# A decoder layer on one Trainium2 core: masked scores kept in PSUM, transposes ahead of scores, and a rebuilt passage from the last head group into attention

## What is computed

```
x = layernorm(x + mamba(x))                      # 8 groups of 16 heads; each group normed by its own mean square
x = layernorm(x + attention(x, ctx, ctx, mask))  # queries x, keys and values ctx
x = layernorm(x + (silu(x @ Wg.T) * (x @ Wu.T)) @ Wd.T)

def attention(q, k, v, mask):                    # 32 query heads of 16, 8 key heads
    scores = einsum('bsgrd,btgd->bgrst', q, k) / sqrt(16) + mask
    probs = softmax(scores, axis=-1)
    return einsum('bgrst,btgd->bsgrd', probs, v)
```

## Time and profile before

| | us |
|---|---|
| median of 3 runs | 1650.11 (1648.63 to 1650.75) |
| the profiled execution | 1650.3 |
| its span | 1648.6 |
| PE busy | 1612.6 (98%) |
| DVE busy | 1197.8 (73%) |
| ACT busy | 950.9 (58%) |
| POOL busy | 962.6 (58%) |

### The profile page before, as it was taken

The page is one execution under the profiler, slowest core; times in us unless marked ns, Lnnn a source line. Parts: engine busy times, 40 slices in busy tenths (PEclk is TensorE's granted clock), DMA queues, the critical chain, the costliest instruction groups (busy, mean ns, idle before and its releaser), DMA issues.

```text
span 1648.6 us, 25601 instructions
## 1 busy us (share of the span) xinstructions
PE 1612.6 (98%) x9120; PEld 1271.4 (77%) x9120; DVE 1197.8 (73%) x2366; ACT 950.9 (58%) x1584; POOL 962.6 (58%) x727
## 2 busy tenths in 40 slices
PE   8999999999999999999999999999999997889998
PEld 7788888888888888888888888888888884444646
DVE  7767688767877786768686868586858679996433
ACT  6765377446745583558364837384738365995231
POOL 2977478657956694759474948495938563330000
PEclk9999999999999999999999999999999999999999
DMA  5432133213412241224131423142314182000000
GB/s 187 148 114 78 58 103 134 77 58 102 132 61 78 90 135 58 90 85 134 53 101 61 135 74 103 53 140 62 119 45 135 58 107 106 1 20 20 13 14 26
DMA packets 76547, 138.85 MB, mean 84 GB/s; under 512 B 6786, under 2 KB 13954, under 8 KB 76164
## 3 DMA queue, kind: packets, MB, share of 16 engines
q1 hardware_dynamic: 76420, 137.21, 26.5%
HBM read 134.55 MB, written 2.63 MB: 83 GB/s over the span
## 4 chain that ended last, share of the span: by engine, by line
PE 90%; DVE 6%; issue 1%; ACT 1%; DMA 1%; POOL 0%; SPq 0%; DVEq 0%; POOLq 0%; ACTq 0%
PE ps_hs L248 8%; PE ps_hs L250 8%; PE ps_hs L249 8%; PE ps_gate L249 8%; PE ps_gate L248 8%; PE ps_gate L250 8%; PE ps_y L1199 7%; PE ps_hs L1207 7%; PE ps_hs L1208 7%; PE ps_hs L1209 7%; PE ps_gate L1183 4%; PE ps_y L1487 3%; PE ps_hs L1449 3%; PE ps_dec L1449 3%; DVE pr L1030 2%
## 5 line engine op out<-in xcount | busy, mean ns | idle before, releaser
L765 DVE SCALAR_TENSOR_TENSOR conv<-ps_hs,cw,conv 128x508 f32<-128x508 f32 (+2 forms) x432 | 320.1, 741 | 31.5 <-ACT conv L530 20.2
L394 POOL TENSOR_TENSOR cum_bc<-cum_bc,neg_cum 128x1024 f32<-128x1024 f32 x128 | 247.5, 1934 | 10.8 <-DMA cum_bc<-cum_scratch 0.2
L248 PE MATMUL ps_hs<-x_hi,w_hi 128*128 128x512 f32 x576 | 231.4, 402 | 0.0
L250 PE MATMUL ps_hs<-x_hi,w_lo 128*128 128x512 f32 x576 | 225.2, 391 | 0.0
L248 PE MATMUL ps_gate<-x_hi,w_hi 128*128 128x512 f32 x576 | 224.4, 390 | 0.0
L249 PE MATMUL ps_hs<-x_lo,w_hi 128*128 128x512 f32 x576 | 224.3, 389 | 0.0
L249 PE MATMUL ps_gate<-x_lo,w_hi 128*128 128x512 f32 x576 | 224.3, 389 | 0.0
L250 PE MATMUL ps_gate<-x_hi,w_lo 128*128 128x512 f32 x576 | 224.3, 389 | 0.0
L1207 PE MATMUL ps_hs<-wo_hi,g_hi 128*128 128x512 f32 x488 | 190.3, 390 | 0.0
L1209 PE MATMUL ps_hs<-wo_hi,g_lo 128*128 128x512 f32 x488 | 190.0, 389 | 0.0
L1208 PE MATMUL ps_hs<-wo_lo,g_hi 128*128 128x512 f32 x488 | 189.9, 389 | 0.0
(11 more groups left out here) (172 smaller groups left out, 3240.6 us busy)
## 6 DMA issues: line engine op xcount, KB each, us to landing
cum_bc<-cum_scratch SPq DMA_DIRECT2D x128, 512.0 KB, 4.2
w_raw<-w_in SPq DMA_DIRECT2D x145, 256.0 KB, 4.7
wo_raw<-w_out SPq DMA_DIRECT2D x64, 256.0 KB, 5.0
g_acc<-x_t SPq DMA_DIRECT2D x4, 512.0 KB, 6.8
acc<-x_nat SPq DMA_DIRECT2D x1, 2048.0 KB, 10.1
k_rep<-ctx_t SPq DMA_DIRECT2D x8, 256.0 KB, 12.9
out<-y_out SPq DMA_DIRECT2D x8, 256.0 KB, 2.0
wg_sb<-w_gate SPq DMA_DIRECT2D x1, 1792.0 KB, 17.2
```

Of the source, the lines that this page charges most:

```text
L248: eng.matmul(ps, whi, xhi, start=(k == 0), stop=False)
L250: return eng.matmul(ps, wlo, xhi, start=False, stop=(k == n - 1))
L394: gp.tensor_tensor(part, part, start.broadcast_to([P, 2, HB, SEQ]), ALU.add).then_inc(S["bc_ok"], 1)
L765: v.scalar_tensor_tensor(out=dst, in0=src, scalar=cw[:, at, TAPS - 1 - n:TAPS - n], in1=dst, op0=ALU.mult, op1=ALU.add).then_inc(S["tap"], 1)
```

## The change

**Scores.** `masked` writes back into its own score bank instead of `pr`, and `exponentials` reads there and writes `pr`. So the bank is free only after the exponential: `scores(i)` waits for `p_exp` of i - 2, half by half, where it waited for `s_max` of i - 2.

**Order.** In the loop PE issues `values` and `turn_probs` ahead of `scores`; ACT issues `keep_queries` after the first half's exponentials instead of before; `scores(0)` stands ahead of the last batch's `last_products`.

**Statistics.** `first_stats` of batches 2 to 7 move from before the loop into its iterations 0 to 5, and `second_part(7)` into iteration 0 between the two halves. The reciprocal roots, other than of batches 0 and 1 and of the last norm, are now made on POOL (`powers`: add EPS, then a power of -0.5) inside its loop of `k_bd`; ACT's roots with their table loads go, and one small exponential loads the table ahead of the loop.

**Last group.** `earlier_squares` moves up behind the last output products, into `ps_dec[0]`, and `last_squares` up in front of most products; the first sum is taken early, the mask is negated early.

```
@@ DVE, ahead of the loop
+            dve.wait_ge(S["ss_early"], 1)
+            v.tensor_scalar(rstd_g[:, :], ps_dec[0][:, 0:BATCH], 1.0 / (TPG * P), EPS, ALU.mult, ALU.add)\
+                .then_inc(S["ss_part"], 1)
+            dve.wait_ge(S["m3_in"], 16)
+            v.tensor_scalar(mask_sb[:, :], mask_sb[:, :], -1.0, None, ALU.mult).then_inc(S["m3_neg"], 1)
+            dve.wait_ge(S["ss_part"], 1)
             dve.wait_ge(S["ss_ps"], GROUPS)
-            v.tensor_scalar(rstd_g[:, :], ps_y[0][:, 0:BATCH], 1.0 / (TPG * P), EPS, ALU.mult, ALU.add)\
-                .then_inc(S["ss_part"], 1)
...
-            for n in range(2):
-                normed(1, n, acc[:, n, :]).then_inc(S["x1_ok"], 1)
-            for b in range(3, 6):
+            normed(1, 0, acc[:, 0, :]).then_inc(S["x1_ok"], 1)
+            for b in range(3, 5):
                 first_part(b)
                 second_part(b)
+            normed(1, 1, acc[:, 1, :]).then_inc(S["x1_ok"], 1)
+            first_part(5)
+            second_part(5)
             first_part(6)
             first_part(7)
-            first_stats(2)
             second_part(6)
-            first_stats(3)
-            second_part(7)
-            for b in range(4, BATCH):
-                first_stats(b)
-            variances(1, 1, others)
@@ DVE, in the loop
             def masked(i, par):
                 dve.wait_ge(S["s_ps"], 2 * i + par + 1)
-                need(dve, S["pt_ps"], 2 * (i - 3) + par + 1)
+                need(dve, S["p_exp"], 2 * (i - 3) + par + 1)
                 for r in range(REP):
                     n = par * REP + r
+                    one = S_PS[i % 2][par][:, r * SEQ:(r + 1) * SEQ]
                     last = v.tensor_tensor_reduce(
-                        out=pr[i % 3][:, n, :], in0=S_PS[i % 2][par][:, r * SEQ:(r + 1) * SEQ], in1=mask_sb[:, :],
+                        out=one, in0=one, in1=mask_sb[:, :], scale=1.0, scalar=FAR, op0=ALU.add, op1=ALU.min,
...
                     masked(i, 0)
+                    if i == 0:
+                        second_part(7)
                     masked(i, 1)
-                if i == 1:
-                    inverses(1, 1, others)
+                if i + 2 < BATCH:
+                    first_stats(i + 2)
@@ ACT
             def exponentials(i, par):
                 act.wait_ge(S["s_max"], 2 * i + par + 1)
+                need(act, S["pt_ps"], 2 * (i - 3) + par + 1)
-                    e = sc.activation(pr[i % 3][:, n, :], pr[i % 3][:, n, :], ACT.Exp, scale=-1.0,
-                                      bias=neg_max[:, i % 3, n:n + 1])
+                    e = sc.activation(pr[i % 3][:, n, :], S_PS[i % 2][par][:, r * SEQ:(r + 1) * SEQ], ACT.Exp,
+                                      scale=-1.0, bias=neg_max[:, i % 3, n:n + 1])
...
-            root(1, 1, slice(2, BATCH))
+            sc.activation(rstd[2][:, 0:1], ones[:, 0:1], ACT.Exp).then_inc(S["exp_table"], 1)
...
-                if i == 23:
-                    root(2, 0, slice(0, HB))
...
-                    if hf == 0 and m == 3:
-                        root(2, 1, slice(HB, BATCH))
@@ POOL
+            def powers(stage, cols):
+                pool.wait_ge(S[f"mv{stage}"], cols.stop)
+                gp.tensor_scalar(rstd[stage - 1][:, cols], mv[stage - 1][:, cols, 1], EPS, None, ALU.add)\
+                    .then_inc(S[f"eps{stage}"], 1)
+                pool.wait_ge(S[f"eps{stage}"], 1 + (cols.stop == BATCH))
+                gp.tensor_tensor(rstd[stage - 1][:, cols], rstd[stage - 1][:, cols], minus_half[:, cols], ALU.pow)\
+                    .then_inc(S[f"pow{stage}"], 1)
...
+                if i == 3:
+                    powers(1, slice(2, HB))
+                if i == 7:
+                    powers(1, slice(HB, BATCH))
+                if i == 24:
+                    powers(2, slice(0, HB))
...
+            powers(2, slice(HB, BATCH))
@@ PE
             outputs(t, 1)
+            earlier_squares(t)
             pe.wait_ge(S["wo_lo_ok"], t)
-            last_products((0, 1, 2, 3), (2,))
-            earlier_squares(t)
+            last_products((0,), (2,))
             last_squares(t)
...
             def scores(i):
-                need(pe, S["s_max"], 2 * (i - 2) + 2)
                 for par in range(2):
+                    need(pe, S["p_exp"], 2 * (i - 2) + par + 1)
```

More of the change, by code:

```diff
@@ L409, in _ @@
             gp.tensor_copy(ones_r[:, :], ones[:, :]).then_inc(S["ones_r_ok"], 1)
+            gp.memset(minus_half[:, :], -0.5).then_inc(S["half_ok"], 1)
+            pool.wait_ge(S["half_ok"], 1)
             def split_squares(g):
@@ L1117, in _ @@
                         batch_done(BATCH - 1)
-                        variances(2, 1, second_half)
                     if m == 4:
-                        inverses(2, 1, second_half)
+                        dve.wait_ge(S["pow2"], 2)
                     if m in (4, 5):
@@ L1267, in earlier_squares, with last_squares @@
                 pe.wait_ge(S["sq_add"], 2 * t)
+                for b in range(BATCH):
+                    mm = pe.matmul(ps_dec[0][:, b:b + 1], sq_acc[:, b * SEQ:(b + 1) * SEQ], ones[:, 0:1],
+                                   start=True, stop=True)
+                mm.then_inc(S["ss_early"], 1)
+            def last_squares(t):
+                pe.wait_ge(S["sq_ok"], 2 * t + 2)
                 pe.wait_ge(S["g_lo_ok"], 2 * t + 1)
                 for b in range(BATCH):
-                    pe.matmul(ps_y[0][:, b:b + 1], sq_acc[:, b * SEQ:(b + 1) * SEQ], ones[:, 0:1],
-                              start=True, stop=True)
-            def last_squares(t):
-                pe.wait_ge(S["sq_ok"], 2 * t + 2)
-                for b in range(BATCH):
-                    mm = pe.matmul(ps_y[0][:, BATCH + b:BATCH + b + 1],
+                    mm = pe.matmul(ps_y[0][:, b:b + 1],
                                    sq_tmp[:, b // HB, (b % HB) * SEQ:(b % HB + 1) * SEQ], ones[:, 0:1],
@@ L1418, in _ @@
             last_products((6,), range(TPH))
+            pe.wait_ge(S["rstd_v"], GROUPS)
+            scores(0)
             pe.wait_ge(S["gacc_ok"], kept + 4)
@@ L1421, in _ @@
             pe.wait_ge(S["v_ok"], 1)
-            pe.wait_ge(S["rstd_v"], GROUPS)
-            scores(0)
             pe.wait_ge(S["gacc_ok"], kept + 6)
@@ L1427, in _ @@
                     pe.wait_ge(S["gacc_ok"], kept + BATCH)
-                if i + 1 < CHUNKS:
-                    scores(i + 1)
                 if i % 2 and i >= 5:
@@ L1433, in _ @@
                     turn_probs(i - 2)
+                if i + 1 < CHUNKS:
+                    scores(i + 1)
                 if i % 2 and i >= 7:
@@ L1452, in hidden @@
                     mm.then_inc(S[done], 1)
-            pe.wait_ge(S["s_max"], 2 * CHUNKS)
+            pe.wait_ge(S["p_exp"], 2 * CHUNKS)
             pe.wait_ge(S["x2_lo_ok"], HB)
```

29 lines of the change are left out of this document (14 added, 15 removed).

## The result

The changed kernel is slower by 0.3%: 1654.15 us, median of 7 runs (1652.77 to 1658.19), against 1649.12 of before in the same comparison (7 runs). The ratio is 1.003 with a 95% interval of 1.002 to 1.0039. In all that follows two executions that ran slow at a lower granted clock (2709.19 us of e7_first, 1802.77 of e11_best) are left out of medians and ratios.

What follows compares the result with a forecast made beforehand. Three nearly full engines were taken to hold each other up in the attention loop; 1370.2 + 101.3 + 2.6 + 2.5 put the last mask at 1476.6, 8.1 us earlier, giving 1642.0 us, range 1638.5 to 1649.

Steps and rivals of the forecast that it cites:

- Part 1: Last sums of squares ahead of the loop: sum ready 1.65 us earlier, one small operation gone, 1.9 us in all.
- Part 2: DVE up to the first mask: statistics and small work leave, 6.35 us saved; first mask at 1370.2.
- Part 3: ACT in the loop: exponentials from PSUM 0.04 us shorter, table loads gone; work per batch from 12.7 to 11.3 us.
- Part 4: DVE in the loop bounds next: 101.3 us of work, plus 10 ns per PSUM mask, 2.6 us for 256.
- Rival 3: DVE's PSUM masks in the loop each cost 20 to 40 ns more: 1644.5 to 1649.5 us, chance 0.12.
- Part 5: Score ring and PE's queue in the loop: 3 us of slack, DVE idle 2.5 us in place of 10.0.
- the note on POOL: POOL in the loop: 4.16 us of work in 13.9, small operations 1 to 2 us ahead of need; cost 0.
- POOL's power: Power instruction on POOL, without a row: up to 1.5 us each covered, cost taken as 0.
- DVE's list: DVE's loop work by kind: 95.5 us before, 101.3 with six statistics and batch 7's addition.
- The stretch behind the last mask: From last mask to the FFN's first matmul: 7.1 us of turned probabilities and split x2, unchanged.
- The rule named in the prediction: Memory latency shows between VectorE and ScalarE instructions; by it ACT's saving is real and DVE's 256 short masks pay each time.

Runs made afterwards that it cites:

- e7_first: Changed kernel with masked scores back in SBUF, bank freed by the mask, and PE's old loop order (scores ahead of values and transposes): 1644.4 us, ratio 0.9971.
- e11_best: Changed kernel with masked scores in SBUF, POOL's key blocks beside the masks, and three products instead of one between the sums of squares: 1640.7 us, ratio 0.9946.
- e4_order: Changed kernel with PE's loop order undone: scores ahead of values and transposes, PSUM output and release by the exponentials kept: 1713.6 us, ratio 1.0385.
- e8_table: Changed kernel with a table of DVE operations, alone and beside POOL, behind its last store: 1692.2 us, of which only the table's rows count.
- e2_keys: Changed kernel with one more wait on POOL, so its key blocks are multiplied beside DVE's masks: 1647.7 us, ratio 0.9992.
- e1_sbuf: Changed kernel with masked scores back in SBUF, exponentials in place there and the score bank freed by the mask: 1641.8 us, ratio 0.9963.
- e10_share: Changed kernel, masks still in PSUM, with key blocks beside masks, three products between squares, and ACT copying half 1 of every fourth piece: 1646.1 us, ratio 0.9978.
- e9_bboth: Kernel before with the scores part alone: masks in PSUM, scores released by both halves' exponentials, values and transposes ahead of scores: 1664.1 us, ratio 1.0089.

## Why the prediction was wrong, step by step

Two steps failed. The price of the mask's output in PSUM was put at 10 ns and measured 31 on average (5.7 us in all), and POOL's multiplications beside DVE's operations in SBUF had no term at all (6.8 us). A smaller one is the clock at the last squares (1.4 us). The last mask was to end at 1476.6 and ended at 1490.07, 13.5 us later. The terms:

- **Part 1 (last squares), size wrong.** The additions were to start 1.9 us earlier, at 1354.2; they started at 1355.57, 1.4 us late. The order of work did what was said. The run of e4_order, where the clock held through the second set, has the step at 2.86, 1.98 less than before. I took the 1.93 us of the earlier trace rows for a set that now stands nearly alone behind another, and did not ask what clock it would have.
- **Part 2 (DVE up to the first mask), right.** From first addition to first mask 15.83 us; 1370.2 less 1354.2 is 16.0. With part 1's error the first mask came at 1371.4.
- **Part 3 (ACT), right.** Exponentials from PSUM stand 0.25 us apart instead of 0.29, ACT is busy 12.18 in 15.0 us and waits for DVE (13.3 us in 13 waits in the loop). Worth what the next engine lets through, as it said.
- **Part 4 (DVE late next), right on the engine and wrong on two sizes.** The bound is DVE, full. The price of the mask was put at 10 ns from a plain multiplication in place, 19 ns in the earlier trace rows. That row was true for what it showed, and e8_table finds no price on a plain addition; but the mask is another kind of instruction, and its price was 38 ns from one to the next, 31 on average since the first of a row of masks has none (in the table the second starts 0.21 us behind the first, into PSUM as into SBUF). Masks cost 62.3 instead of 54.0 + 2.6: 5.7 us. Rival 3 (20 to 40 ns) had this size with a chance of 0.12 and would by itself have given 1647.7 (1642.0 + 5.7), still faster than before.
- **Parts 4 and 5, a term missing: POOL beside DVE.** Normed rows 4.0 us and additions 2.8 us longer, 6.8 in all. No part and no rival had it. Part 2 itself named the effect for the two normed rows (2.39 us, "POOL was multiplying keys beside them"), and the note on POOL in part 5 asked only whether POOL has time, not at which of DVE's instructions it would run once its release (the scores) had moved. It took both terms to make the kernel slower: without this one (e2_keys) it is level with the one before, and without the mask's price (e1_sbuf) it is faster.
- **Part 5 (ring and queue), right in size, by luck.** DVE's idle was to be 2.5 in place of 10.0, and by the same reading (length less busy, 118.70 and 115.92) it was 2.8. But the waits that the part laid out, masks 0.3 to 0.6 us in front of late scores once for each batch, did not come: 1.1 us is one wait for batch 7's products, the rest gaps of under 0.15 us. DVE was too full to wait for scores. Once it was lighter (e10_share) they came, 4.0 us in six waits. The small figure also held only with PE's new order and ACT's: in e9_bboth, without the queries' copy behind the first exponentials and the release by halves, the column has 10.2, and with scores in front (e4_order) 63.7.
- **POOL's power,** taken as covered: 0.73 and 1.03 us for 128 x 2 and 128 x 4, and nobody waited on it in the loop.
- All other terms of DVE's list (copies, statistics and the rest) came 0.5 us below it.

The first mask came 1.2 us late. DVE was busy 115.92 us where the list with the mask's price had 103.9, so 12.0 more: 5.7 and 6.8, less 0.5. Idle was 0.3 more. That is 13.5, as measured. The stretch behind the last mask was taken as unchanged (7.1) and was 5.6. Of eight transposes there, those of the kernel before took 1.91 us:

```profile
1486.61 1.91 PE L1378 MATMUL ps_gate<-ident,pr 128*128 128x128 f32 x8
```

and those of the changed kernel 1.04, at full clock (1.00 for the stretch, 0.76 in the earlier trace rows):

```profile
1491.74 1.04 PE L1396 MATMUL ps_gate<-ident,pr 128*128 128x128 f32 x8
```

That is chance of the clock more than the change: the same kernel with the table behind it has the long end again (7.1 us, clock 0.76, eight transposes in 1.91). So 12.0 us of 13.5 remain, and 1642.0 and 12.0 are the 1654 that were measured.

The rule named in the prediction, the Trainium skill's Read-Write Bubble ("Advanced Engine Details and Errata"), pointed the right way for this instruction, read as the prediction reads it: short tiles into PSUM pay each time on VectorE. Read so, it would also have charged the plain additions, and for these the table has no difference (1.67 and 1.69 us for eight). And the row on POOL has its rule, which no part of the prediction used: the Trainium skill ("SBUF — State Buffer", Who interferes with whom) says that a scalar operation in its two-port form, or one of two tensors both in SBUF, shares a port pair with GpSimd, and that whichever issues first holds it. By it normed rows and additions are hit, and masks and copies from PSUM are not. The table agrees for the first three (4.38 and 4.68 against 1.43, masks unchanged), and in the changed kernel's loop copies out of PSUM take 0.67 to 0.68 us with POOL beside them or without. On who holds it the rows go a little further: POOL's record starts 0.09 us behind DVE's in the rows that DVE lost (1427.43 and 1427.52), and 0.35 us behind in those that it kept (e1_sbuf).

What stays open: what in the chip lengthens the accumulator read behind an output in PSUM (139 ns against 83), and whether it is this read that spaces the masks. Only that the price goes with the place of the output, and that a plain addition doesn't have it, is shown. Open too is what brings the clock down at the squares: that more wide products between the sets go with a full clock is shown, not why. And what the moved statistics, the powers on POOL and the queries' copy are worth one by one was not run.

## What to carry to other kernels

Take a price only from a row of the same instruction form: the plain operation and the one with an accumulated output differed by 5.7 us over 256 of them, out of a gain of 8. When a transfer of work moves what releases another engine, lay that engine's instructions along the timeline of its neighbour again, because "it has time" says nothing about whom it will stand beside; the repair is one wait. And a release that is moved to a later event needs the queue around it rebuilt with it: against before, the release by the exponential stood at 14 us more with ACT's part of the order and the release by halves missing (e9_bboth, which also lacks the rest of the change) and at 64 with PE's missing (e4_order).

## What the runs showed of the hardware

- A 128 x 128 sum with row minimum on DVE takes 0.211 us from one to the next with its output in SBUF and 0.249 in PSUM, whatever the source; a plain sum of that size 0.21 in both.
- An exponential of 128 x 128 on ACT costs 0.25 us from one to the next from PSUM (changed kernel) and 0.29 in place in SBUF (before, e1_sbuf).
- Beside POOL's multiplication a 128 x 512 scaling in SBUF goes from 0.36 to 1.10 us, a 128 x 256 sum of SBUF operands from 0.36 to 1.17. POOL starting 0.09 us after the DVE instruction still held it up (1427.43 and 1427.52 above); 0.35 us after, it did not, and took 1.09 us itself instead of 1.04 (e1_sbuf).
- With sixteen one-column products, three wide ones and sixteen again the granted clock of PE fell from 1.00 to 0.50 (the level of 1.2 GHz) in all seven kernels that had them, for 3.4 to 10.2 us; with nine wide ones between it stayed at 1.00 in all three. With both sets back to back, twelve wide ones ahead, as in the kernel before, it stayed at 1.00 through the sets in both profiles, and in e9_bboth fell 1 us behind them.
- In e4_order, where PE waited 45 times in the loop, 0.2 to 1.4 us each, the granted clock was 0.84 over the loop; in the changed kernel it was 0.99.
